# A quantised feed-forward: x and h transposed by DMA, x's statistics on ScalarE, x's division moved

## What is computed

```python
h = _layernorm(x, axis=-1) * (1 + cb) + sb
x = x + gb * _L0_ffn_ref(h, w_gate, w_up, w_down)      # inner width 1408

def fp4_quant_dequant(x):       # blocks of 16 along the last dim
    scale = jnp.maximum(jnp.max(jnp.abs(xb), axis=-1, keepdims=True) / 6.0, 1e-12)
    idx = jnp.searchsorted(_MID, jnp.abs(xb / scale))
    return _GRID[idx] * jnp.sign(xb / scale) * scale
gate, y = fp4_linear(x, w_gate), fp4_linear(x, w_up)   # both operands quantised
return fp4_linear(silu(gate) * y, w_down)
```

## Time and profile before

| | us |
|---|---|
| median of 3 runs | 4235.33 (4228.73 to 4249.51) |
| the profiled execution | 4212.4 |
| its span | 4210.4 |

### The profile page before, as it was taken

One profiled execution on the slowest core, in us unless ns is written; L12 is line 12 of the kernel. 1 busy time (PEld: TensorE's weight loads), 2 busy tenths in 40 slices (PEclk: granted clock), 3 DMA queues, 4 the chain that ended last, 5 costly groups with the idle time before them and its releaser, 6 DMA issues. The chain is left out here.

```text
span 4210.4 us, 155629 instructions
## 1 busy us (share of the span) xinstructions
PE 3699.2 (88%) x65992; PEld 2513.7 (60%) x65992; DVE 3525.5 (84%) x7798; ACT 1608.1 (38%) x3173; POOL 1142.4 (27%) x736
## 2 busy tenths in 40 slices
PE   4989898888988988888898943699999999999998
PEld 3767677676776767767677732355555555455554
DVE  4888878878887887878888859799999999999997
ACT  2434344343443534434344313233333333333333
POOL 1122212222212221222222215333333333333332
PEclk7999999999999999999999976799999999999999
DMA  4000000000000000010000030011101111111110
GB/s 116 13 26 25 24 28 18 29 23 24 28 19 28 23 24 28 19 33 18 24 28 19 18 125 10 23 31 36 34 31 39 31 39 31 39 31 34 36 31 31
DMA packets 73617, 133.45 MB, mean 32 GB/s; under 512 B 13248, under 2 KB 14016, under 8 KB 72896
## 3 DMA queue, kind: packets, MB, share of 16 engines
q1 hardware_dynamic: 72896, 123.13, 9.2%
HBM read 89.56 MB, written 33.55 MB: 29 GB/s over the span
## 5 line engine op out<-in xcount | busy, mean ns | idle before, releaser
L764 POOL TENSOR_TENSOR raw_up<-raw_up,raw_gate 128x1024 f32<-128x1024 f32 x128 | 312.3, 2440 | 1077.4 <-DVE raw_up L814 1077.4
L932 DVE COPY_PREDICATED Am<-pick,banks 128x64 f32<-128x64 uint8 (+2 forms) x1792 | 461.4, 257 | 127.7 <-DVE Am L932 12.4
L1647 PE MATMUL fbank<-dT,hqT 128*128 128x512 f16 x2112 | 488.8, 380 | 20.8 <-ACT hqT L1564 20.8
L1635 PE MATMUL fbank<-gT,xqT 128*128 128x464 f16 (+1 forms) x2304 | 490.9, 363 | 11.4 <-issue 6.6
L1635 PE MATMUL fbank<-uT,xqT 128*128 128x464 f16 (+1 forms) x2304 | 487.7, 361 | 0.0
L530 PE MATMUL banks<-raw_up,raw_gate 128*128 128x256 f32 x2048 | 457.5, 382 | 1.8 <-DVE xxx L827 1.8
L530 PEld LDWEIGHTS banks<-raw_up,raw_gate 128*128 128x128 f32 x2048 | 385.5, 191 | 53.7 <-issue 2.1
L775 POOL TENSOR_TENSOR yrs<-yvar,neg_half 128x32 f32<-128x32 f32 x32 | 174.0, 5437 | 819.8 <-DVE yvar L961 819.8
L1575 ACT ACTIVATE sil<-fbank,und 128x464 f32<-128x464 f32 (+1 forms) x192 | 124.0, 646 | 655.0 <-PE fbank L1635 655.0
L1635 PEld LDWEIGHTS fbank<-gT,xqT 128*128 128x128 f16 x2304 | 225.6, 98 | 248.3 <-issue 12.6
L1635 PEld LDWEIGHTS fbank<-uT,xqT 128*128 128x128 f16 x2304 | 225.5, 98 | 231.1 <-issue 0.4
(11 more groups left out here) (235 smaller groups left out, 7686.9 us busy)
## 6 DMA issues: line engine op xcount, KB each, us to landing
raw_scale<-in_L_attn_x SPq DMA_DIRECT2D x32, 512.0 KB, 3.7
xres<-in_L_attn_x SPq DMA_DIRECT2D x32, 512.0 KB, 3.6
x_after_attention<-xres SPq DMA_DIRECT2D x32, 512.0 KB, 3.6
xl<-x_after_attention SPq DMA_DIRECT2D x64, 256.0 KB, 2.8
xr<-x_after_attention SPq DMA_DIRECT2D x64, 256.0 KB, 2.7
out<-xr SPq DMA_DIRECT2D x64, 256.0 KB, 2.0
raw_gate<-in_L_ffn_w_gate SPq DMA_DIRECT2D x1, 2816.0 KB, 11.4
raw_up<-in_L_ffn_w_up SPq DMA_DIRECT2D x1, 2816.0 KB, 18.9
```

Of the source, the lines that this page charges most:

```text
L764: nc.gpsimd.tensor_tensor(xf[:, j % NXF].rearrange("p g b t -> p (g b) t"), xf[:, j % NXF].rearrange("p g b t -> p (g b) t"), hT[:, :, :, ...
L932: nc.vector.copy_predicated(dst, mask, src).then_inc((done or A_step).sem, 1)
L1635: last = nc.tensor.matmul(GU[2 * pair + t][:, 0:w], xqT[:, u, a, g, :], W[:, b_, g, lo_:hi_], start=(k == 0), stop=(k == 3 * G - 1))
L1647: last = nc.tensor.matmul(DN[1 - u][:], hqT[:, a, kk, :], dT[:, b_, kk, :], start=(first and kk == 0), stop=(end and kk == KF - 1))
```

## The change

Three things at once, all in the feed-forward.

PE makes no transposes any more and ScalarE no copies of them. SP issues three transposing DMAs per tile from SBUF to SBUF: xq of tile n+1, both parts at once, when its low part is done; the high part of hq of tile n when it is done; the low part when POOL has made it. They stand in sp_body between the loads and the store, all in SP's queue. hqT gets a second stage, and PE waits for the landings.

Mean and variance are made by ScalarE (act_stats): a pass with an accumulated sum, the negated mean, a pass of squares with an accumulated sum, and the variance plus epsilon, four instructions between the second and the third Silu. bn_stats, bn_aggr and the two that follow leave DVE.

quantise is cut in two at Q_SCALED: divide (maxima, scale, reciprocal, division) and the rest. In dve_body divide of x for tile n+1 stands ahead of the first third of h of tile n, the rest of it behind that third as before; for h the two follow each other. turn_go is raised ahead of each transposing DMA and nothing waits for it.

```diff
-        TR = bank[4:6]
...
+        hqT = sb("hqT", [P, 2, 2, KF, P], F16)
...
+        def divide(dve, n, w, src, s, inv, pw, step):
+
+            blocks, bc, k, link = chain(dve, n, w, step, 0)
             V = nc.vector
...
+            assert k[0] == Q_SCALED
+
+        def quantise(dve, n, w, src, m, q, s, s16, pw, step, grid_done, dst, done, freed, q_free, scales=None):
+
+            blocks, bc, k, link = chain(dve, n, w, step, Q_SCALED)
...
-        def sp_body(sp, j, u, n, do_m, do_out, more):
-            if more:
+        def sp_xT(sp, u, n):
+            after(sp, xq_done, n)
+            after(sp, xlow_done, n)
+            after(sp, gu_done, n - 2)
+            sp.sem_inc(turn_go.sem, 1)
+            sp.dma_start_transpose(xqT[:, u].rearrange("p a g t -> p (a g) t"), xq[:].rearrange("p a n -> p (a n)")).then_inc(xT_landed.sem, 16)
+
+        def sp_hT(sp, u, n):
+            after(sp, hq_done, n)
+            after(sp, down_done, n - 2)
+            sp.sem_inc(turn_go.sem, 1)
+            sp.dma_start_transpose(hqT[:, u, 0], hq[:, 0]).then_inc(hT_high.sem, 16)
+            after(sp, hlow_done, n)
+            sp.sem_inc(turn_go.sem, 1)
+            sp.dma_start_transpose(hqT[:, u, 1], hq[:, 1]).then_inc(hT_low.sem, 16)
+
+        def sp_body(sp, j, u, n, do_m, do_out, more, loads):
+            if loads:
                 after(sp, ln_done, n)
                 b, ts_ = tile_of(j + 1, u)
                 sp.dma_start(xl[:, u], x1[b, ts_, :]).then_inc(xl_loaded[u].sem, 16)
...
+            if more:
+                sp_xT(sp, 1 - u, n + 1)
+            if do_m:
+                sp_hT(sp, u, n)
             if do_out:
...
-        def dve_ln(dve, j, u, n):
-
-            after(dve, xl_loaded[u], j)
-            nc.vector.bn_stats(stats[:, u], xl[:, u]).then_inc(st_done.sem, 1)
-
-        def dve_ln2(dve, u, n):
-            settled_then(dve, all_max.sem, st_done, n)
-            nc.vector.bn_aggr(mv[:, u], stats[:, u]).then_inc(mv_done.sem, 1)
-            after(dve, mv_done, n)
-            nc.vector.tensor_scalar(negmu[:, u:u + 1], mv[:, u, 0:1], -1.0, None, ALU.mult)
-            nc.vector.tensor_scalar(ve[:, u:u + 1], mv[:, u, 1:2], EPS, None, ALU.add).then_inc(ve_done.sem, 1)
...
+        def dve_xa(dve, u, n):
             after(dve, mod2, n)
-            quantise(dve, n, C, hx[:], mx[:], q16x, sx, ix, s16x, xp[:, u], xstep, xgrid_done, xq, xq_done, lambda: after(dve, xT_done, n - 1),
+            divide(dve, n, C, hx[:], sx, ix, xp[:, u], xstep)
...
+        def dve_xq(dve, u, n):
...
-            quantise(dve, n, I_FF, h[:, u], mh[:], q16h, sh, ih, s16h, hp[:, u], hstep, hgrid_done, hq, hq_done, lambda: after(dve, hT_done, n - 1),
+            divide(dve, n, I_FF, h[:, u], sh, ih, hp[:, u], hstep)
+            quantise(dve, n, I_FF, h[:, u], mh[:], q16h, sh, s16h, hp[:, u], hstep, hgrid_done, hq, hq_done, lambda: (after(dve, hT_high, n - 1), after(dve, hT_low, n - 1)),
...
-            jn = j if u == 0 else j + 1
+            if more:
+                dve_xa(dve, 1 - u, n + 1)
             if do_m:
                 dve_h(dve, u, n, 0)
             if more:
-                dve_xq(dve, jn, 1 - u, n + 1)
+                dve_xq(dve, 1 - u, n + 1)
             if do_m:
                 dve_h(dve, u, n, 1)
-            if two_more(n):
-                dve_ln(dve, j + 1, u, n + 2)
-                dve_ln2(dve, u, n + 2)
-            if do_m:
                 dve_h(dve, u, n, 2)
...
+        def act_stats(act, j, u, n):
+            after(act, xl_loaded[u], j)
+            nc.scalar.activation(passed[:], xl[:, u], ACT.Identity, accum_out=sums[:, u, 0:1]).then_inc(sum_done.sem, 1)
+            after(act, sum_done, n)
+            nc.scalar.activation(negmu[:, u:u + 1], sums[:, u, 0:1], ACT.Copy, scale=-1.0 / C).then_inc(negmu_done.sem, 1)
+            after(act, negmu_done, n)
+            nc.scalar.activation(passed[:], xl[:, u], ACT.Square, bias=negmu[:, u:u + 1], accum_out=sums[:, u, 1:2]).then_inc(square_done.sem, 1)
+            after(act, square_done, n)
+            nc.scalar.activation(ve[:, u:u + 1], sums[:, u, 1:2], ACT.Identity, bias=eps[:], scale=1.0 / C).then_inc(ve_done.sem, 1)
...
-        def act_xT(act, u, n):
-            after(act, xT_done, n)
-            after(act, gu_done, n - 2)
-            nc.scalar.activation(xqT[:, u].rearrange("p a g t -> p (a g t)"), TR[0][:].bitcast(F16), ACT.Copy).then_inc(xT_used.sem, 1)
...
-            if do_out:
-                act_hT(act, n - 1, 0)
-                act_hT(act, n - 1, 1, u)
-            if more:
-                act_xT(act, 1 - u, n + 1)
-            if do_out:
-                act_hT(act, n - 1, 2)
+                    if s == 1 and two_more(n):
+                        act_stats(act, j + 1, u, n + 2)
             if two_more(n):
                 act_ln(act, u, n + 2)
-            if do_out:
-                act_hT(act, n - 1, 3)
             if do_m:
...
-                        after(pe, xT_used, n)
+                        after(pe, xT_landed, n)
...
             if do_out:
-                m = n - 1
-                pe_hT(pe, m, 0, None)
-                pe_hT(pe, m, 1, None, u)
-                if more:
-                    pe_xT(pe, 1 - u, n + 1)
-                def down(ks, a, b_, first=False, end=False):
-                    for kk in ks:
-                        last = nc.tensor.matmul(DN[1 - u][:], hqT[:, a, kk, :], dT[:, b_, kk, :], start=(first and kk == 0), stop=(end and kk == KF - 1))
+                m, v = n - 1, 1 - u
+
+                def down(a, b_, first=False, end=False):
+                    for kk in range(KF):
+                        last = nc.tensor.matmul(DN[v][:], hqT[:, v, a, kk, :], dT[:, b_, kk, :], start=(first and kk == 0), stop=(end and kk == KF - 1))
                     return last
-                after(pe, hT_used, m, 1)
-                down(range(4), 0, 0, first=True)
-                after(pe, hT_used, m, 2)
-                down(range(4, 8), 0, 0)
-                pe_hT(pe, m, 2, None)
-                down(range(8), 0, 1)
-                pe_hT(pe, m, 3, n + 1 if more else (n if do_m else m))
-                after(pe, hT_used, m, 3)
-                down(range(8), 1, 0)
-                after(pe, hT_used, m)
-                down(range(8, KF), 0, 0)
-                down(range(8, KF), 0, 1)
-                down(range(8, KF), 1, 0, end=True).then_inc(down_done.sem, 1)
-            elif more:
-                pe_xT(pe, 1 - u, n + 1)
+                after(pe, hT_high, m)
+                after(pe, scaled_out, m - 2)
+                down(0, 0, first=True)
+                down(0, 1)
+                after(pe, hT_low, m)
+                down(1, 0, end=True).then_inc(down_done.sem, 1)
...
+                    act_stats(act, 0, 0, 0)
                     act_ln(act, 0, 0)
+                    act_stats(act, 0, 1, 1)
```

More of the change, by code:

```diff
@@ L1374, in feed_forward @@
         xlow_done, hlow_done = sig("xlow_done", 1), sig("hlow_done", 1)
-        xT_done, xT_used = sig("xT_done", 1), sig("xT_used", 1)
-        hT_done, hT_used = sig("hTf_done", 4), sig("hTf_used", 4)
+        xT_landed = sig("xT_landed", 1, 16)
+        hT_high, hT_low = sig("hT_high", 1, 16), sig("hT_low", 1, 16)
+        turn_go = sig("turn_go", 3)
         gu_done, sil_done, h_done = sig("gu_done", 3), sig("sil_done", 3), sig("h_done", 3)
@@ L1387, in tile_of, with chain @@
             return u, bass.ts(j, P)
-        def quantise(dve, n, w, src, m, q, s, inv, s16, pw, step, grid_done, dst, done, freed, q_free, scales=None):
+        def chain(dve, n, w, step, k0):
             nb = w // NB
@@ L1393, in quantise @@
             bc = lambda ap: ap.unsqueeze(2).to_broadcast([P, nb, NB])
-            k = [0]
+            k = [k0]
             def link(ins):
@@ L1399, in link @@
                 after(dve, step, n, k[0])
+            return blocks, bc, k, link
+        def divide(dve, n, w, src, s, inv, pw, step):
+            blocks, bc, k, link = chain(dve, n, w, step, 0)
             V = nc.vector
@@ L1522, in pool_xlow @@
         def pool_xlow(pool, n):
-            low_part(pool, n, C, q16x, s16x, xq_done, xq, xlow_done, lambda: after(pool, xT_done, n - 1))
+            low_part(pool, n, C, q16x, s16x, xq_done, xq, xlow_done, lambda: after(pool, xT_landed, n - 1))
         def pool_body(pool, j, u, n, do_m, do_out, more):
@@ L1530, in pool_body @@
             if do_m:
-                low_part(pool, n, I_FF, q16h, s16h, hq_done, hq, hlow_done, lambda: after(pool, hT_done, n - 1))
+                low_part(pool, n, I_FF, q16h, s16h, hq_done, hq, hlow_done, lambda: after(pool, hT_low, n - 1))
             if do_out:
@@ L1546, in act_grid @@
             nc.scalar.activation(m, src, ACT.Abs, bias=grid_shift[:], scale=GRID_SCALE).then_inc(done.sem, 1)
-        def act_xT(act, u, n):
-            after(act, xT_done, n)
-            after(act, gu_done, n - 2)
```

(20 more changed lines are left out.)

44 lines of the change are left out of this document (7 added, 37 removed).

## The result

The changed kernel takes 4257.3 us (median of 20 runs, 4237.77 to 4273.2), the kernel before 4233.26 (20 runs, 4221.79 to 4251.66): ratio 1.0049, 95% interval 1.0035 to 1.0064. It is slower by half a per cent, where 1% faster was forecast.

The account below looks back on a forecast made before the run. PE was taken as the bound, DVE just behind. Two loops of 22.8 and 22.75 us replace 23.57 a tile: 47 us on 62 periods, less 1.5 at the ends, giving a median of 4189 us, range 4140 to 4540.

Parts of the forecast that it names:

- The bound before: In the feed-forward, PE is the bound, busy 490 of 500 us, with DVE at 467; one tile takes 23.57 us.
- Loop A: From h2 through h's quantisation, x's division and h0 on DVE to PE's third slice and Silu: 22.8 us a tile.
- the 47 forecast: Gain in the feed-forward: 23.57 - 22.8 = 0.77 us on 62 periods, 47 us, before the ends.
- 0.1 for what POOL's two operations: Term of Loop A: POOL's operations on hx hold up DVE's maximum and division of h by 0.1 us, bounds nothing to 1.4.
- I take that they go: On DVE, the 1.41 us a tile that two short steps on h lose to POOL were assumed to disappear.
- Loop B: Through SP's queue: h's low transpose, store, load of xl, ScalarE's statistics, third Silu, back to h2: 22.75 us a tile.
- the 1.3 named as the least: Lowest time in us for h's low transpose in Loop B, since the store waits for POOL's add anyway.
- Rival 1: Transposing DMAs take long in SP's queue, making the kernel slower: 4535 us at 5 us, 4783 at 7.0; chance 0.35.
- The ends: At the feed-forward's ends, the first x waits longer for its statistics and landing: 1.5 us given back.
- rival 2: Gain eaten: statistics take 2.9 us, or POOL holds h's division up by a microsecond: 4215 to 4255; chance 0.15.

Follow-up runs that it names:

- e8: The kernel before with only the transposing DMAs of the change, statistics and x's division as before: 4192.35 us, ratio 0.9921.
- e2: The changed kernel with POOL's add to hx made to wait until DVE has passed h's scale step: 4201.74 us, ratio 0.9942.
- after: The changed kernel itself, with all three parts of the change, against the kernel before: 4257.3 us, ratio 1.0049.
- e1: The changed kernel with h's first third ahead of x's division again on DVE: 4188.03 us, ratio 0.9908 to the kernel before.
- e6: The changed kernel with only ScalarE's third Silu put ahead of the statistics: 4308.77 us, ratio 1.0176 to the kernel before.
- e7: The kernel before with only x's division moved ahead of h's first third on DVE: 4282.18 us, ratio 1.013.
- e9: The kernel of e2 with a fourth transposing DMA per tile in SP's queue, into an unread buffer: 4311.12 us, ratio 1.0176 to the kernel before.
- e4: The changed kernel with six unread matmuls of 512 columns ahead of PE's third slice: 4233.8 us, ratio 1.0025 to the kernel before.
- e5: The kernel of e1 with ScalarE's third Silu put ahead of the statistics: 4128.05 us, ratio 0.976 to the kernel before.
- e10: The kernel of e5 with POOL's two operations on x held until step 11 of h's chain: 4186.65 us, ratio 0.9887 to the kernel before.
- e3: The changed kernel with mean and variance on DVE again, ScalarE's four instructions gone: 4245.09 us, ratio 1.0042 to the kernel before.

## Why the prediction was wrong, point by point

- **The bound before** was read rightly: PE, with DVE close behind. e8 shows that taking the transposes off PE brings 0.8% (0.9921), with DVE the bound at once.
- **Loop A** was right but for one term: 22.8 forecast, 22.88 in the undisturbed tile, with the wait of 1.32 us (forecast 1.3) for h0 and L1409 on 32 columns at 1.20 (forecast 1.1). By this tile alone the change would have brought (23.57 - 22.89) x 62 = 42 us of the 47 forecast.
- **The step that failed** is the term "0.1 for what POOL's two operations, now beside h's maximum and division, hold up there (nothing to 1.4 us)". The two were placed rightly, but the term was taken near its lower bound with nothing to choose it by. It measured 1.10 us in 28 tiles and 0.83 in 13: 42 us, as much as the gain above. e2, which takes this race away and pays 0.28 us a tile for it, is at 0.9942, or 0.6% faster.
- **What had no term**: the clock. A longer pause was taken as a wait and nothing more; behind 12 waits it cost some 1.6 us each, 19 us in all. Together 61 us are lost against a gain of 42: 19 (17 if the one such fall in the kernel before is taken off), where 18.2 were measured.
- **DVE's waits for POOL.** "I take that they go" was half right: L1426 and L1427 take 0.27 and 0.25 in after (1.41 us gone), and L1409 gives 1.1 of it back in two tiles of three. The prediction also named a rule of the Trainium skill ("SBUF — State Buffer", "Who interferes with whom"), that the two engines exclude each other for a whole instruction, and drew from it that such waits move with the order and are not shortened by it. The exclusion is borne out at each meeting shown here. What was drawn from it holds from before to after: what DVE's instructions take beyond their undisturbed length is 2.3 us a tile before and 2.1 after. It does not hold in general: in e1 it is 1.2, in e2 1.7, in e6 2.8 and in e7 2.9. The order sets the sum.
- **Loop B**: 22.75 forecast, level with loop A; e9 puts it some 0.4 us below. Its terms: the statistics 2.13 (2.0); a transpose lands in 3.1 us, but SP, which is what the loop goes through, is held for 1.36 only, nearest to the 1.3 named as the least (1.7 taken). Rival 1, the slow transposes, did not happen; e9 shows that from one more issue on it would have. The Trainium skill's figure of 1,309 ns for one 128x128 block ("VectorE: DVE Perf Modes", three transpose paths), taken in series as the prediction did, does not describe what was measured: 11 blocks land in 3.1 us, 0.28 us a block.
- **The ends**: 1.5 us forecast, 22.2 - 20.7 = 1.5 measured up to the first matmul. Beyond it the sum had no terms, and they nearly cancel: the first two intervals take 51.1 us against 45.2 before, the last one 19.0 against 23.6.
- **The rivals.** The one that came true is the second half of rival 2 (POOL holds up h's division by a microsecond), and with the clock behind it it went beyond the 4215 to 4255 given there. Not asked at all was whether the change is better without its third part. The same sum could have told: by rows 4 and 5 h0 comes 3.6 us later through the move, loop A is shorter without it, and e1 and e7 put it at 1.3 to 1.4% in both kernels.

What stays open: why the clock falls behind 11 of 29 long pauses and not the others, and what makes the tiles at each end of a lap of ten long (24 to 26.5 us in most kernels, the one before included, up to 27.8 in e4). That e5's gain over e1 comes from the Silu's place alone is shown; how much POOL still costs there is not, as e10 only made it worse.

## What to carry to other kernels

An operation that another engine waits for goes ahead of one that nobody waits for yet: compare each part of a change with the change without it, not only with the kernel before. Where two engines exclude each other, an edit that frees time also shifts where they meet, by fractions of a microsecond; give such a meeting its whole price in the sum unless the order is fixed by a wait, and then look whether the fixed order is really cheap. In-order queues decide what new work costs: in e1 four statistics instructions ahead of the third Silu cost 1.0 us a tile, which putting them behind it gave back (e5). The same move in the other order was a loss (e6), so this too is to be tried in the order at hand.

## What the runs showed of the hardware

- A race of 0.05 us between a DVE and a POOL instruction (0.03 ahead or 0.02 behind) is worth 1.1 us. In after the winner alternates over long stretches of tiles; that the longer tile shifts the next meeting is likely, but no run isolates it.
- The exclusion works both ways and on float16 operands too: POOL's 1.26 became 2.71 and 2.52, DVE's 1.62 became 2.57.
- TensorE's granted clock went to 0.50 behind some pauses: in after behind 12 of 30 from 2.25 us on, in e6 behind 18 of 61 from 2.55 on, at the shortest behind 1.98 (e3); in e2, where nearly all were 1.56 or 1.67, only behind the one of 8.0. With 1.46 us of filling work in the pause ahead of the third slice it fell there in the second tile alone, where 7.2 us of pause were left (e4).
- A transposing DMA from SBUF to SBUF holds SP for 1.24 to 1.37 us, against 0.33 to 0.53 for a plain one, and lands in 2.7 (x) and 3.1 us (half of h). A sum on ScalarE by accumulation adds an instruction of 0.19 us to the pass.
